# Halves of the shared expert's rows made beside the norm and transposed by the DMA engines

## The reference, cut to what matters

```python
x = x + tanh(g_xattn[0]) * L0_xattn(ctx, ctx, layernorm(x), ssm_kernel, D)     # long convolution
xn = layernorm(x)
logits = xn @ router_w.T                                  # then softmax, top 2 of 8
shared = silu(xn @ s_gate_w + s_gate_b) * (xn @ s_up_w + s_up_b) @ s_down_w + s_down_b
x = x + tanh(g_ffn[0]) * (moe_out + shared)
x = x + tanh(g_xattn[1]) * L1_xattn(layernorm(x), ctx, ...)                    # linear attention
x = x + tanh(g_ffn[1]) * L1_ffn(layernorm(x), ...)                             # soft mixture of 16 experts
```

## Time and profile before

| | |
|---|---|
| median of the three runs | 1817.76 us |
| profiled execution, its own time | 1817.87 us |
| its span, first to last instruction | 1816.1 us |
| mean granted TensorE clock over the span | 0.943 |
| share of the span busy: PE, DVE, ACT, POOL | 87%, 60%, 42%, 29% |
| busy in 253 to 510 us (257.0 us): PE, DVE, ACT, POOL | 224.8, 134.8, 88.5, 82.1 us |

### The profile page before, as it was taken

One profiled execution on the slowest core, in us unless ns is written; L12 is line 12 of the kernel. 1 busy time (PEld: TensorE's weight loads), 2 busy tenths in 40 slices (PEclk: granted clock), 3 DMA queues, 4 the chain that ended last, 5 costly groups with the idle time before them and its releaser, 6 DMA issues. The chain is left out here.

```text
span 1816.1 us, 27604 instructions
## 1 busy us (share of the span) xinstructions
PE 1583.9 (87%) x9596; PEld 925.9 (51%) x9596; DVE 1083.5 (60%) x2154; ACT 754.6 (42%) x1390; POOL 519.0 (29%) x428
## 2 busy tenths in 40 slices
PE   2879985999979999777898984979999999999997
PEld 1668872444446666434453542445555555555554
DVE  4778854543632223277676857566767767675664
ACT  2543213333412233144343431465565646565462
POOL 2347850434422344333434332101102020101101
PEclk6889997999989999978999997989999999999999
DMA  9435545433475665353515124651432505142341
GB/s 191 96 92 144 160 137 178 134 110 111 153 208 147 175 180 150 121 199 116 159 63 162 59 93 149 260 108 42 88 68 60 110 23 121 23 104 52 65 85 44
DMA packets 274042, 215.18 MB, mean 118 GB/s; under 512 B 184514, under 2 KB 222914, under 8 KB 272274
## 3 DMA queue, kind: packets, MB, share of 16 engines
q1 hardware_dynamic: 232640, 152.53, 31.9%
q10 hardware_dynamic: 32034, 31.10, 5.9%
q0 software_dynamic: 9264, 30.15, 5.5%
HBM read 120.33 MB, written 49.63 MB: 94 GB/s over the span
## 5 line engine op out<-in xcount | busy, mean ns | idle before, releaser
L2018 POOL TENSOR_TENSOR s_h_lo<-s_h,s_h_hi 128x512 f16<-128x512 f32 x32 | 36.9, 1154 | 554.2 <-DVE s_h_hi L2229 554.2
L1205 DVE TENSOR_TENSOR e_h<-e_up,e_silu 128x352 f32<-128x352 f32 x39 | 20.5, 525 | 149.8 <-ACT e_silu L1164 146.5
L511 PE MATMUL ring<-prod_hi,toep 128*128 128x288 f16 x320 | 94.7, 296 | 13.5 <-DVE terms L431 12.9
L299 POOL TENSOR_TENSOR prod_lo<-prod,prod_hi 128x2304 f16<-128x2304 f32 x16 | 73.3, 4584 | 107.2 <-ACT prod_hi L341 107.2
L2247 PE MATMUL s_ring<-w_mu,s_xt_hi 128*128 128x512 f16 x256 | 98.7, 386 | 4.2 <-DVE s_xt_lo L2150 3.9
L2249 PE MATMUL s_ring<-w_mu,s_xt_lo 128*128 128x512 f16 x256 | 98.5, 385 | 0.0
L2248 PE MATMUL s_ring<-w_mu,s_xt_hi 128*128 128x512 f16 x256 | 98.4, 384 | 0.0
L2247 PE MATMUL s_acc<-w_w,s_g_hi 128*128 128x512 f16 x256 | 97.1, 379 | 0.1
L2247 PE MATMUL s_ring<-w_w,s_xt_hi 128*128 128x512 f16 x256 | 97.0, 379 | 0.0
L2248 PE MATMUL s_ring<-w_w,s_xt_hi 128*128 128x512 f16 x256 | 97.0, 379 | 0.0
L2249 PE MATMUL s_ring<-w_w,s_xt_lo 128*128 128x512 f16 x256 | 97.0, 379 | 0.0
(11 more groups left out here) (376 smaller groups left out, 4771.0 us busy)
## 6 DMA issues: line engine op xcount, KB each, us to landing
expert_rows<-e_y SPq DMA_DIRECT2D x39, 256.0 KB
toep<-ssm_split ACTq DMA_DIRECT2D x16, 512.0 KB
a_part_in<-in_L_ffn_W ACTq DMA_DIRECT2D x32, 256.0 KB
w_split<-a_part_q ACTq DMA_DIRECT2D x32, 256.0 KB, 2.5
w_w<-w_split SPq DMA_DIRECT2D x8, 1024.0 KB, 15.5
stage<-in_L_ffn_gate_w SPq DMA_DIRECT2D x8, 704.0 KB
stage<-in_L_ffn_up_w SPq DMA_DIRECT2D x8, 704.0 KB
c_rows<-in_ctx SPq DMA_DIRECT2D x8, 512.0 KB
```

What stands on the lines that cost most here:

```text
L299: nc.gpsimd.tensor_tensor(prod_lo[:, u].rearrange("p k e r -> p (k e r)"), prod[:, u, :], prod_hi[:, u].rearrange("p k e r -> p (k e r)"), ...
L511: nc.tensor.matmul(out, w_hi, hi, start=(n == 0), stop=False)
```

## The change

For chunks 1 to 3 the halves of the rows are made once, as rows, and the DMA engines transpose them. In chunk 0 all stays as it was.

- xt_hi and xt_lo become the two halves of one tensor xt, eight blocks wide.
- ScalarE splits the high half of the four tiles of chunk c+1 (`split_rows`) right after the square root of that chunk's norm, no longer between the blocks of chunk c+1. Before tile 0 it waits for the row store of the chunk before and for its transposes, both of which read xq.
- VectorE makes the four low halves (`rest_of_rows`) right after the norm and ahead of the four output additions of chunk c.
- SyncE waits until the last gate and up matmul of chunk c has read xt, then issues one DMA transpose for each tile as its low half is done, then the row store of chunk c+1. Only chunk 0's row store stays where it was.
- TensorE no longer transposes in chunks 1 to 3, ScalarE and VectorE no longer copy tr to xt there. The first gate matmul waits for the DMA transposes (xq_turned). The waits on bias_added that stood ahead of the transposes, and kept tr from being overwritten, now stand ahead of the router's matmuls, of the rank matmuls and of each tile of the down product.
- VectorE's wait ahead of writing xn is needed for chunk 1 alone, on TensorE's transposes of chunk 0.

```diff
@@ shared_phase, tensors
-        xt_hi, xt_lo = (lent(KD * CH).rearrange("p (k i) -> p k i", k=KD) for _ in range(2))
+        xt = lent(2 * KD * CH).rearrange("p (k i) -> p k i", k=2 * KD)
+        xt_hi, xt_lo = xt[:, 0:KD, :], xt[:, KD:2 * KD, :]
@@ SyncE
+            def store_xn(c):
+                sp.wait_ge(xq_lo_done, (c + 1) * 4)
+                sp.dma_start(xn_d[:, c * 4:c * 4 + 4, :], xq.rearrange("p t q d -> p t (q d)")).then_inc(xn_stored, 16)
...
-                sp.wait_ge(xq_hi_done, (c + 1) * 4)
-                sp.wait_ge(xq_lo_done, (c + 1) * 4)
-                sp.dma_start(xn_d[:, c * 4:c * 4 + 4, :], xq.rearrange("p t q d -> p t (q d)")).then_inc(xn_stored, 16)
+                if c == 0:
+                    store_xn(0)
                 if c < LAST:
                     for i in range(2):
                         sp.wait_ge(ew_lo, c * 4 + i + 3)
                         load_piece(c + 1, i)
+                    sp.wait_ge(gu_done, (c + 1) * SK)
+                    for t in range(4):
+                        sp.wait_ge(xq_lo_done, (c + 1) * 4 + t + 1)
+                        sp.dma_start_transpose(xt[:, :, t * P:(t + 1) * P], xq[:, t, :, :].rearrange("p q d -> p (q d)")).then_inc(xq_turned, 16)
+                    store_xn(c + 1)
@@ ScalarE
+            def split_rows(c, t):
+                if not t and c:
+                    act.wait_ge(xn_stored, c * 16)
+                    act.wait_ge(xq_turned, (c - 1) * 4 * 16)
+                act.wait_ge(normed, c * 4 + t + 1)
+                nc.scalar.activation(xq[:, t, 0, :], xn[:, t, :], ACT.Copy).then_inc(xq_hi_done, 1)
...
-                if c:
-                    split_turned(c)
...
-                        if m == 0 and c:
-                            act.wait_ge(xn_stored, c * 16)
-                        act.wait_ge(normed, c * 4 + m + 1)
-                        nc.scalar.activation(xq[:, m, 0, :], xn[:, m, :], ACT.Copy).then_inc(xq_hi_done, 1)
+                        if c == 0:
+                            split_rows(0, m)
...
                 if c < LAST:
                     ln.root(nc, act, c + 1)
+                    for t in range(4):
+                        split_rows(c + 1, t)
@@ VectorE
-                if c:
-                    dve.wait_ge(xq_lo_done, c * 4)
+                if c == 1:
+                    dve.wait_ge(turned, KD)
...
+            def rest_of_rows(c, t):
+                dve.wait_ge(xq_hi_done, c * 4 + t + 1)
+                V.tensor_tensor(xq[:, t, 1, :], xn[:, t, :], xq[:, t, 0, :], ALU.subtract).then_inc(xq_lo_done, 1)
...
-                if c:
-                    rest_of_turned(c)
...
-                    if 1 <= m <= 4:
-                        dve.wait_ge(xq_hi_done, c * 4 + m)
-                        V.tensor_tensor(xq[:, m - 1, 1, :], xn[:, m - 1, :], xq[:, m - 1, 0, :], ALU.subtract).then_inc(xq_lo_done, 1)
+                    if c == 0 and 1 <= m <= 4:
+                        rest_of_rows(0, m - 1)
...
                 if c < LAST:
                     normalise(c + 1, 1 - c % 2)
+                    for t in range(4):
+                        rest_of_rows(c + 1, t)
                     for t in range(4):
                         add_out(c, t)
@@ TensorE
-                for b in range(KD):
+                for b in range(KD if c == 0 else 0):
                     for t in range(4):
                         if b == 0:
-                            pe.wait_ge(normed, c * 4 + (t + 1))
-                        if t == 0 and c:
-                            pe.wait_ge(bias_added, (c - 1) * 4 + (b + 1))
+                            pe.wait_ge(normed, t + 1)
...
-                            if m == 0 and o == 0:
-                                pe.wait_ge(xt_lo_done, c * KD + (b + 1))
+                            if m == 0 and o == 0 and c == 0:
+                                pe.wait_ge(xt_lo_done, b + 1)
+                            if m == 0 and o == 0 and c and b == 0:
+                                pe.wait_ge(xq_turned, c * 4 * 16)
...
                     if m == 0:
+                        if c:
+                            pe.wait_ge(bias_added, (c - 1) * 4 + 1)
...
                     if c == LAST and m == 2:
                         pe.wait_ge(picked_done, 1)
+                        pe.wait_ge(bias_added, c * 4)
...
                 for t in range(4):
                     tok = slice(t * P, (t + 1) * P)
+                    if c:
+                        pe.wait_ge(bias_added, (c - 1) * 4 + t + 1)
```

More of the change, by code:

```diff
@@ L617, in shared_phase @@
         xt_hi_done, xt_lo_done = sem("xt_hi_done"), sem("xt_lo_done")
-        xq_hi_done, xq_lo_done = sem("xq_hi_done"), sem("xq_lo_done")
+        xq_hi_done, xq_lo_done, xq_turned = sem("xq_hi_done"), sem("xq_lo_done"), sem("xq_turned")
         routed, logits_read = sem("routed"), sem("logits_read")
```

## The result

| | before | after |
|---|---|---|
| median of six runs on one chip | 1817.11 us (1811.44 to 1821.31) | 1805.93 us (1803.52 to 1810.14) |
| ratio | | 0.9938, 95% interval 0.9921 to 0.9955 |
| span of the profiled execution | 1816.1 us | 1806.9 us |

The shared phase does what the prediction says; the surplus comes from another phase.

The account below looks back on a forecast made before the run. TensorE, busy for 87% of the 1816.1 us span, was taken as the bound. Three seams save 7.0 us, all else 0: span 1809.1 us, forecast time 1810.8 us, range 1808.0 to 1816.0 us.

Parts of the forecast that it names:

- The seam: Between chunks of the shared expert, removing TensorE's 48 transposes saves 2.34, 2.34 and 2.33 us, 7.0 us in all.
- Whether the halves are ready: First seam: last DMA transpose lands at 350.7, needed at 351.83; cost taken as 0, at most 10.7 us in all.
- The spare of 1.1 us: First seam: time between the last DMA transpose's landing at 350.7 and the first gate matmul's need at 351.83.
- The edits costed at nothing: Shared expert: moved bias_added waits, later output additions, fewer ScalarE and VectorE operations and the moved row store; taken as 0.
- Rival 1: At the seams the halves come late in part; gain 2.5 to 5.5 us, time 1812.3 to 1815.3; chance 0.17.
- rival 3: The seam closes but the time comes back, say in the expert phase's start; 1815 to 1818 us; chance 0.10.
- All that follows: After the shared phase, everything starts from its earlier end and keeps its length, so the 7.0 us reaches the end.
- Rival 4: Fewer VectorE and GpSimd collisions win a little more than the seam: 8 to 9 us, 1809 to 1810; chance 0.04.

Follow-up runs that it names:

- pe_padded: The changed kernel plus 48 unread matmuls of eight columns at the end of the shared phase's TensorE program; 1808.82 us, ratio 0.9964 to before.
- one_by_one: The changed kernel, but SyncE waits for each DMA transpose to land before issuing the next; 1818.11 us, ratio 1.003 to before.
- store_first: The changed kernel with the 1 MB row store issued ahead of the four DMA transposes; 1812.54 us, ratio 0.9988 to before.
- rows_only: The kernel before with only the early row splits and row store; TensorE's transposes and their copies stay; 1812.72 us, ratio 0.9997 to before.
- before_p80: The kernel before plus 80 tiny unread matmuls (160 instructions) at the end of the shared phase; 1810.53 us, ratio 0.9977 to before.
- after_p128: The changed kernel plus 128 tiny unread matmuls (256 instructions) at the end of the shared phase; 1804.34 us, ratio 0.9934 to before.
- after_p96: The changed kernel plus 96 tiny unread matmuls (192 instructions) at the end of the shared phase; 1805.39 us, ratio 0.9938 to before.

## Why the prediction was wrong

**The seam, right.** Three seams of 2.34, 2.34 and 2.33 us: the phase is 7.0 us shorter in the means, and pe_padded, with most of the surplus taken out, gains 6.5.

**Whether the halves are ready, right in order and size.** Shifted by the 1.1 us, the first issue was forecast at 344.6 and came at 344.37. The four issues took 1.44 us apiece (5.77/4) against 1.3. Landing was put at 3.3 us from a tile of the same size; it is 2.8 in the median, 3.7 at most. The last issue starts at 348.82 and lands 2.8 us later, at 351.65; TensorE needs it at 352.97. That leaves 1.3 us, and 1.8 and 0.95 at the other two seams. The spare of 1.1 us was a fair estimate, and one_by_one and store_first show what stands behind it: about 8.3 and 7.5 us. The Trainium skill's price for DMA transposes (1309 ns a block, "VectorE: DVE Perf Modes", section "The three transpose paths"), which the prediction weighed and set aside, isn't borne out: eight blocks land in 2.8 us.

**The edits costed at nothing, right.** The waits on bias_added, the moved additions and the moved splits show in no row, and rows_only puts the last at nothing. Rival 1 (late in part) and rival 3 (given back in the expert phase) didn't come: the expert phase is 257.8 to 258.4 us against 258.7.

**The step that failed: "All that follows (the barrier, the gathers of rows, the expert phase) starts from that end and keeps its length."** It starts from that end. But the soft mixture doesn't keep its length; it lost 3.8 us. The sum lacked a term, and the range, with 1808.0 as its lower end, no room for it. The mechanism, as far as the runs carry it: TensorE's program is 97 instructions shorter, so its 16 KB fetches fall at other points of the soft mixture. Before, some fall where SyncE issues one transpose after another. The transposes in flight then land 4.5 us and more behind their issue in place of 3.3, ScalarE waits for such a landing before it can write s_eq again, VectorE falls behind with it, and TensorE ends up waiting. (The issue that is on the queue at that moment takes 1.8 to 2.3 us in place of 1.27, a mark of the same meeting, not its price.) The signs were in the rows: the landing of 4.9 us and the issue of 2.33 in the earlier trace rows both stand at such a meeting (1684.9 and 1687.6 us, fetch at 1687.38), but the prediction used them only as bounds for its own transposes. Three things show it: without the change but with the fetches where after has them, the time falls by 4.2 us (before_p80); with the change but the fetches where before has them, most of the surplus goes (pe_padded); and a shift by one whole fetch changes nothing (after_p128). 6.5 and 4.2 add to 10.7, against 11.2, 10.7 and 12.0 measured for the whole. Rival 4 had the right sign, with collisions between VectorE and GpSimd as its cause, which no row supports.

The Trainium skill bears on this in "Runtime: NRT & Kernel Launch", section "Instruction fetch mechanics": instructions are refilled by DMA in blocks of 16 KiB (256 instructions), and it calls the crossing mostly hidden. The trace agrees on the size (66 packets, 1.08 MB) and on the 256 (255 records between fetches), though it shows no fetch for 4,400 records. It agrees on "mostly" in that nearly all of the 66 cost nothing that we found, but the few that meet a dense row of transposes cost 4 us together.

**Left open.** Why a fetch lengthens a transpose's landing and issue, and which exact distance hurts: after_p96 has slow issues for free, and before_p80 has a fetch in its last stretch too. About 1 us of attention goes the other way and wasn't pursued.

## What to carry to other kernels

Costing an edit phase by phase gives its own effect; adding or removing instructions also moves the instruction fetches of everything behind, which was worth 4 us of 1816 here, so a range below half a per cent needs that term with both signs. To tell the two apart, run a control with the count restored by cheap instructions in an idle place, and compare the lengths of phases over several profiles rather than two spans. A path that's hidden by about 1 us is hidden by its order: make the kernel with the wrong order once, to know what the cover is worth.

## What the runs showed of the hardware

- Four DMA transposes of 128x1024 fp16 from one queue overlap: issued 1.3 to 1.8 us apart, each landing 2.7 to 3.7 us after its issue. Waiting for each landing makes four take 10.29 us of issue time in place of 5.77 (one_by_one).
- A 16 KB instruction fetch that falls among packed transposes goes with slower ones: the one being issued takes 1.6 to 2.4 us in place of 1.23 to 1.43 (33 of 1792, every one within 0.52 us of a fetch), and transposes in flight can land 4 to 5 us behind their issue in place of 3.3 (81 of the 99 landings over 4 us in the soft mixtures have such a fetch between issue and landing).
- Idle time of TensorE sometimes cost more than itself: right behind a wait of 2.5 us in one_by_one (402.5 us) and one of 2.0 us in store_first (354.6 us) stands a stretch of 3.4 us at the half clock of 1.2 GHz (granted 0.50; matmuls of 634 ns where the others take 380). Four other seam waits of 1.6 to 2.5 us in these two kernels have none.
